# A seven-product output projection in a latent-attention and feed-forward kernel

## The chip, the core and the metric

One core of one Trainium2 chip runs the whole program. The metric is the device time of one execution in microseconds (us). The parts of the core are TensorE (PE, matmuls; PEld is its weight load), VectorE (DVE), ScalarE (ACT), GpSimd (POOL), SyncE (SP, which issues the DMAs here), the on-chip memory SBUF of 128 partitions and the eight accumulator banks of PSUM.

## The reference

For 8 sequences of 512 rows and 512 features (16 heads):

```
h = layernorm(x)
q = rmsnorm(h @ wq_a.T) @ wq_b.T            # latent 384; per head 128 plain + 64 rotary
c, k_pe = split(h @ wkv_a.T); c = rmsnorm(c) # latent 128 + 64 rotary
k, v = split(c @ wkv_b.T)                    # per head 128 + 128
att = softmax((q . [k, rope(k_pe)]) / sqrt(192))
x = x + concat_heads(att @ v) @ wo.T
g = layernorm(x); x = x + (silu(g@gate*s1) * (g@up*s2)) @ down * s3   # weights rounded to fp8, 1536 wide
```

## The kernel before

Each float32 operand of a matmul is split in two f16 halves, high and low, and a product is made of three matmuls (high high, high low, low high: `mul3`, lines 291 to 293). The key and value weights are absorbed once in a setup, so that a head's query (`absorb`, 9 matmuls) meets the latent keys directly, its context is 128 latent values wide (`values`, 12 matmuls, lines 674 to 676) and one matrix per head, `WVO` (128 x 512), takes the context to the output (`project_out`, 4 tiles of 128 rows x 3 matmuls of 512 columns).

The engines run lists written out by hand, held together by semaphores. The batches follow each other: setup, then per batch attention over 16 heads and an FFN of 12 chunks. In `head_step` TensorE does the scores of head i (4 half-height matmuls and 16 full ones, into the four SC banks), the values of head i - 1, the absorption for head i + 2 and the projection of head i - 1. There is one bank, BQ, for absorption. VectorE takes four row maxima (`maxima`), the reciprocals of the sums (`sums_of_head`), splits the context into two halves (`context`), adds the four projected tiles into `XR`, multiplied by the reciprocal of each row's sum (`add_out`, line 1449), and makes the low half of the absorbed query (`qa_lo`). ScalarE makes every exponential twice (`probs`, lines 1077 and 1079): in f32 into `P32`, of which there is one buffer, and in f16 into `PH`; then the high half of the absorbed query (`qa_hi`). GpSimd makes the low halves `PL` = `P32` - `PH` (line 1716), two tiles at a time; the f32 exponentials of the next head wait for it. SP transposes both halves by DMA. The memory of `P32` also holds `YT`, the FFN's output, until GpSimd has added it to the residual (line 1781), at the start of the next batch.

Queries' rotary parts are made in 8 rotations a batch (`rotated_ahead` on TensorE, `rot_products` and `rot_lo` on VectorE, `rotate` on GpSimd, lines 1687 and 1688): 5 beside the FFN before, 3 in the first two heads. At a batch's end (`last_of_attention`) the 8 latents of the next batch (4 of q, 4 of k) fill TensorE's waits: q1, q2, k2 and q3 stand between the last projection and the transposes of the normalised rows (line 557). The last batch has an ending of its own (`end_of_attention`), with 21 filler matmuls (`keep_warm`). The statistics of the next batch's input and its normalised rows (`next_norm`) are made beside heads 3 to 10.

## Time and profile before

| | |
|---|---|
| median of 3 runs | 2231.78 us (2231.71 to 2232.05) |
| the profiled execution | span 2228.8 us; the page gives no other time of it |
| TensorE busy, granted clock | 2205.4 us (99%), 0.999 |
| VectorE, ScalarE, GpSimd busy | 1557.8, 1066.6, 1001.5 us |
| DMA | 219.42 MB, 47.7% of 16 engines in its main queue |

Busy time is a union: overlapping instructions count once. A matmul's own duration (379 ns for 512 columns) is longer than the distance to the next. In timelines and chains the first number is the start from the span's beginning, the second the length.

### The profile page before, as it was taken

What the parts mean: (1) busy time and instruction counts of PE and PEld (TensorE: products, weight loads), DVE (VectorE), ACT (ScalarE), POOL (GpSimd) and SP (SyncE); (2) the same over time, 40 slices, a digit from 0 to 9 for tenths busy, and PEclk for the clock granted to TensorE, in tenths of its full rate; (3) what the DMA queues carried; (4) which work ended last, traced back from release to release, by engine and by line L of the source; (5) the groups of instructions that cost most, each with busy time, mean ns of one, the idle gap of its engine ahead of it and who ended that gap; (6) DMA issues with size and microseconds to landing.
All of it is one profiled execution on the core that took longest, in us unless ns stands there. A gap on an engine that the chain in (4) does not pass through costs nothing.

```text
span 2228.8 us, 34908 instructions
## 1 busy us (share of the span) xinstructions
PE 2205.4 (99%) x10977; PEld 1026.8 (46%) x10977; DVE 1557.8 (70%) x3227; ACT 1066.6 (48%) x2345; POOL 1001.5 (45%) x688
## 2 busy tenths in 40 slices
PE   7999999999999999999999999999999999999999
PEld 5444544445444454444544445444454445444454
DVE  7888887776477764777648775587755877467773
ACT  6667564554255542555325553355443554345532
POOL 4657465453355524454244642536334363343322
PEclk9999999999999999999999999999999999999999
DMA  7868336562175631756216561365614564145530
GB/s 248 188 124 150 88 71 142 106 124 51 23 151 105 122 53 34 145 105 127 44 43 146 106 121 29 73 123 106 118 25 104 106 115 95 24 104 109 106 65 19
DMA packets 703800, 219.42 MB, mean 98 GB/s; under 512 B 685520, under 2 KB 685776, under 8 KB 702672
## 3 DMA queue, kind: packets, MB, share of 16 engines
q1 hardware_dynamic: 703696, 218.09, 47.7%
q8 instruction: 59, 0.97, 0.2%
q14 instruction: 45, 0.37, 0.0%
HBM read 40.78 MB, written 8.39 MB: 22 GB/s over the span
## 4 chain that ended last, share of the span: by engine, by line
PE 93%; DVE 3%; ACT 1%; DMA 1%; POOL 1%; issue 1%; SPq 0%; DVEq 0%; POOLq 0%
PE bank L853 13%; PE bank L291 11%; PE bank L293 11%; PE bank L292 11%; PE scores L863 7%; PE scores L663 5%; PE scores L293 5%; PE scores L291 5%; PE scores L292 5%; PE bank L674 4%; PE bank L675 4%; PE bank L676 4%; PE scores L660 3%; PE bank L840 1%; PE bank L689 1%; PE scores L557 1%
## 5 line engine op out<-in xcount | busy, mean ns | idle before, releaser
L1716 POOL TENSOR_TENSOR arena<-arena 128x1024 f16<-128x1024 f32 x256 | 545.7, 2132 | 620.3 <-ACT arena L1079 620.3
L1077 ACT ACTIVATE arena<-scores,shift 128x512 f32<-128x512 f32 x512 | 357.5, 698 | 535.0 <-DVE shift L1429 494.8
L1449 DVE SCALAR_TENSOR_TENSOR arena<-bank,rden,arena 128x512 f32<-128x512 f32 x508 | 347.9, 743 | 137.0 <-PE bank L293 137.0
L1427 DVE TENSOR_REDUCE mx<-scores 128x1 f32<-128x512 f32 x512 | 352.5, 689 | 20.5 <-PE scores L293 16.7
L1079 ACT ACTIVATE arena<-scores,shift 128x512 f16<-128x512 f32 x512 | 358.6, 700 | 0.0
L853 PE MATMUL bank<-arena,WFF 128*128 128x512 f16 x1392 | 313.5, 379 | 0.8 <-DVE arena L1601 0.6
L1774 POOL TENSOR_TENSOR arena<-arena 128x512 f16<-128x512 f32 x96 | 114.4, 1191 | 255.6 <-ACT arena L1152 255.6
L853 PEld LDWEIGHTS bank<-arena,WFF 128*128 128x128 f16 x1392 | 135.9, 98 | 164.1 <-DVE arena L1601 2.3
L291 PE MATMUL bank<-WVO,arena 128*128 (+1 forms) x512 | 194.2, 379 | 2.4 <-DVE arena L1222 1.2
L1222 DVE SCALAR_TENSOR_TENSOR arena<-bank,arena 128x512 f16<-128x512 f32 (+1 forms) x263 | 176.2, 670 | 29.1 <-ACT arena L1070 24.4
L663 PE MATMUL scores<-arena 128*128 128x512 f16 x512 | 195.4, 382 | 0.0
L292 PE MATMUL bank<-WVO,arena 128*128 (+1 forms) x512 | 194.1, 379 | 0.0
L291 PE MATMUL scores<-arena 128*128 128x512 f16 x512 | 194.0, 379 | 0.0
L292 PE MATMUL scores<-arena 128*128 128x512 f16 x512 | 194.0, 379 | 0.0
L293 PE MATMUL scores<-arena 128*128 128x512 f16 x512 | 194.0, 379 | 0.0
L293 PE MATMUL bank<-WVO,arena 128*128 (+1 forms) x512 | 194.0, 379 | 0.0
L674 PE MATMUL bank<-arena 128*128 128x512 f16 x476 | 180.4, 379 | 1.9 <-DMA arena<-arena 1.7
L676 PE MATMUL bank<-arena 128*128 128x512 f16 x476 | 180.4, 379 | 0.0
L675 PE MATMUL bank<-arena 128*128 128x512 f16 x476 | 180.4, 379 | 0.0
L1441 DVE TENSOR_SCALAR arena<-bank 128x512 f16<-128x512 f32 (+1 forms) x135 | 89.0, 660 | 130.1 <-PE bank L676 125.7
L863 PE MATMUL scores<-WFF,arena 128*128 128x512 f16 x752 | 177.6, 379 | 0.0
L1601 DVE SCALAR_TENSOR_TENSOR arena<-arena,bank 128x512 f32<-128x512 f32 x96 | 65.9, 687 | 158.5 <-ACT arena L1146 158.4
(159 smaller groups left out, 3480.5 us busy)
## 6 DMA issues: line engine op xcount, KB each, us to landing
arena<-arena SPq DMA_TRANSPOSE x712, 3.2
arena<-w_ffn SPq DMA_DIRECT2D x24, 384.0 KB, 3.5
arena<-x SPq DMA_DIRECT2D x8, 1024.0 KB, 5.6
out<-arena SPq DMA_DIRECT2D x32, 256.0 KB, 2.0
arena<-x SPq DMA_DIRECT2D x14, 512.0 KB, 4.4
WVO<-w_o SPq DMA_DIRECT2D x4, 1024.0 KB, 8.2
arena<-w_nope SPq DMA_DIRECT2D x4, 768.0 KB, 9.1
arena<-down_scale SPq DMA_DIRECT2D x8, 256.0 KB, 3.3
```

The lines of the kernel that those rows point to most:

```text
L291: pe.matmul(dst, lhsT=ls(0), rhs=rs(0), start=first, stop=False)
L292: pe.matmul(dst, lhsT=ls(0), rhs=rs(1), start=False, stop=False)
L293: return pe.matmul(dst, lhsT=ls(1), rhs=rs(0), start=False, stop=last)
L663: pe.matmul(dst, lhsT=Q1[:, par, tile(t)], rhs=KA[:, :], start=False, stop=False)
L674: pe.matmul(dst[:, :], lhsT=KV[:, 0, j, :], rhs=PT[:, par, 0, :, j, :], start=(j == 0), stop=False)
L853: m = pe.matmul(dst[:, :], lhsT=w[:, c, k, :], rhs=XT[:, p, k, :], start=(k == 0 and p == 0), stop=(k == NK - 1 and p == 1))
L863: m = pe.matmul(SC[:, t, :], lhsT=FU[:, c % 4, p, tile(t)], rhs=WD[:, c, :], start=(c == 0 and p == 0), stop=(c == NF - 1 and p == 1))
L1077: act.activation(P32[:, t, :], SC[:, t, :], ACT.Exp, scale=EXP_SCALE, bias=shift[:, t:t + 1], accum_out=esum[:, par, t:t + 1]).then_inc(s[ ...
L1079: act.activation(PH[:, par, t, :], SC[:, t, :], ACT.Exp, scale=EXP_SCALE, bias=shift[:, t:t + 1]).then_inc(s["ph"], 1)
L1427: dve.tensor_reduce(mx[:, t:t + 1], SC[:, t, :], AX_X, ALU.max).then_inc(s["mxr"], 1)
L1449: dve.scalar_tensor_tensor(out=XR[:, t, :], in0=banks[t][:, :], scalar=by[:, t:t + 1], in1=XR[:, t, :], op0=ALU.mult, op1=ALU.add).then_in ...
L1716: pool.tensor_tensor(PL[:, par, two, :], P32[:, two, :], PH[:, par, two, :], ALU.subtract).then_inc(s["pl"], 1)
```

## The change

From batch 2 on (`B_PLAIN`), heads 0 to 13 are taken in seven pairs ("duos"). The contexts of a pair (512 rows x 256) times their two matrices (256 x 512) are cut into 2 x 2 blocks and multiplied in seven products of sums of blocks instead of eight (Winograd's form of Strassen's). A product (`duo_product`) is 2 tiles of rows x 3 matmuls of 256 columns. The sums need contexts that are already divided by the row sums, so each head's exponentials are divided: ScalarE makes them once, in f32, then `PH` as a scaled copy and `P32` scaled in place; GpSimd multiplies one tile of four, in heads 0 to 2 two of them (`N_TWO`). GpSimd also sums the blocks of the contexts (`context_sums`, `context_sums_rest`). The sums of the weights' blocks are made in batch 1 by GpSimd and ScalarE (`block_sums`), written to DRAM and loaded for each pair by SP (`early_blocks`, 524 KB, and `late_blocks`, 393 KB); their space on chip is that of `WVO` of heads 0 to 13. The values of head i now come two steps after its scores. Scores wait for `ex`, the f32 exponentials, instead of `ph`. Heads 14 and 15 are projected as before.

Six rotations instead of five are made beside the FFN; of the other two one stays ahead of the scores and one comes after step 1, its halves made by GpSimd (`rotated_halves`). The k latent of tile 2 moves from behind q2 to between the halves of the last values, in all batches but the last. The next input's statistics and rows move, from batch 2's on, to VectorE beside the FFN (`next_norm`, `next_rows`), their halves to ScalarE and GpSimd in heads 4, 6, 8 and 10. The last late weights are issued ahead of one transpose. In the last batch `end_of_attention` interleaves the last two pairs with heads 14 and 15 by halves, and its last down products go tile by tile, tile 3 last; additions of tiles 2 and 3 follow their scaling at once. The FFN's loops, the setup and batches 0 and 1 are otherwise as before.

```diff
+B_PLAIN = 2
...
+EARLY = [(X_E1, W_B11, 0, True), (X_O1, W_B21, 2, True), (X_S1, W_T1, 1, True), (X_S2, W_T2, 0, False)]
+LATE = [(X_S3, W_T3, 0, False), (X_S4, W_B22, 1, False), (X_O2, W_T4, 2, True)]
+ADDS = [(0, 0, 0), (2, 0, 0), (1, 1, 1), (0, 0, 1), (0, 1, 0), (0, 1, 1), (1, 0, 1), (2, 1, 0)]
 CHUNK_ROT = 5
...
-N_ROT_FFN = 5
+N_ROT_FFN = 6
+N_ROT_SETUP = NT + 1
...
+N_TWO = 3
...
-LAST_DOWNS = [(NF - 2, 0), (NF - 2, 1), (NF - 2, 2), (NF - 1, 0), (NF - 1, 1), (NF - 2, 3), (NF - 1, 2), (NF - 1, 3)]
+FIRST_DOWNS = [(NF - 4, 0), (NF - 4, 1)]
+LAST_DOWNS = [(NF - 3, 0), (NF - 3, 1), (NF - 3, 2), (NF - 4, 2), (NF - 2, 0), (NF - 2, 1), (NF - 2, 2),
+              (NF - 1, 0), (NF - 1, 1), (NF - 1, 2), (NF - 4, 3), (NF - 3, 3), (NF - 2, 3), (NF - 1, 3)]
...
+    def duo_head(b, i):
+        if i < NH - 2:
+            sp.wait_ge(s["sp"], NT * (b * NH + i) + NT)
+            rope_rows(i + 2, i % 2)
+        if i == 1:
+            sp.wait_ge(s["rot"], (b + 1) * 2 * N_ROT)
+            sp.sem_inc(s["turn"])
+        if i >= 2:
+            sp.wait_ge(s["ctp"], b * N_CT + i - 1)
+            sp.sem_inc(s["turn"])
+        for half in range(2):
+            prob_rows_hi(b * NH + i, i % 2, half)
+            if half and i == NH - 1:
+                late_blocks(b, N_DUO - 1)
+            prob_rows_lo(b * NH + i, i % 2, half)
...
+    def early_blocks(b, j):
+        if j == 0:
+            sp.wait_ge(s["t_out"], 16 * N_DUO)
+            sp.wait_ge(s["outp"], b * (NH * NT))
+        else:
+            sp.wait_ge(s["outp"], order_of_duo(b, j - 1) + N_EARLY)
+        sp.dma_start(WB[:, :, 0:N_EARLY], w_duo[j, :, :, 0:N_EARLY]).then_inc(s["w_early"], 16)
+    def late_blocks(b, j):
+        if j > 0:
+            sp.wait_ge(s["outp"], order_of_duo(b, j - 1) + 8)
+        sp.dma_start(WB[:, :, N_EARLY:], w_duo[j, :, :, N_EARLY:]).then_inc(s["w_late"], 16)
...
+    def duo_product(j, x, w, bank, start):
+        for t in range(2):
+            dst = bank[:, t * HB:(t + 1) * HB]
+            for m, (p, q) in enumerate(((0, 0), (0, 1), (1, 0))):
+                r = pe.matmul(dst, lhsT=XP[j % 2][:, p, x, tile(t)], rhs=WB[:, q, w, :],
+                              start=(start and t == 0 and m == 0), stop=(m == 2), skip_group_check=True)
+        return r
...
     def end_of_attention(b):
         final = NH // 2 - 1
         scores(b, final, 0)
+        values(b, final - 1, 0)
+        duo_early(b, N_DUO - 2, last=True)
+        scores(b, final, 1)
         values(b, final - 1, 1)
-        scores(b, final, 1)
-        project_out(b, final - 1, 1)
         ph = (b * NH + NH - 1) * NT
-        values_by_halves(b, 0, VBANK_END[0], ((s["qal"], b * NH + NH), (s["outr"], (b * NH + NH - 2) * NT - 1)))
+        values_by_halves(b, 0, (BQ[:, :], BQ[:, :]), ((s["outr"], order_of_duo(b, N_DUO - 2) + 2),))
+        duo_late(b, N_DUO - 2)
         last = ((s["ph"], ph + 1), (s["ph"], ph + 2))
+        values_by_halves(b, 1, VBANK_END[1], last, (0,))
         end_project_out(b, 0, 0)
-        values_by_halves(b, 1, VBANK_END[1], last, (0,))
         end_project_out(b, 0, 1)
+        duo_early(b, N_DUO - 1)
+        pe.wait_ge(s["ph"], ph + NT)
         end_project_out(b, 1, 0)
+        duo_late(b, N_DUO - 1, last=True)
         values_by_halves(b, 1, VBANK_END[1], last, (1,))
         end_project_out(b, 1, 1)
             if t == 2 and final:
...
+    def duo_step(b, i):
+        scores(b, i // 2, i % 2)
+        if i >= 2:
+            values(b, i // 2 - 1, i % 2)
+        if i >= 4 and i % 2 == 0:
+            duo_early(b, (i - 4) // 2, (0,))
+        if i == 5:
+            duo_early(b, 0, (2, 3))
+        absorb(i + 2, b * NH + i + 2)
+        if i >= 4 and i % 2 == 0:
+            duo_early(b, (i - 4) // 2, (1,) if i == 4 else (1, 2, 3))
+        elif i >= 5:
+            duo_late(b, (i - 5) // 2)
...
         absorb(2, base + 2)
-        for n in range(N_ROT_FFN + 1, N_ROT):
+        if b >= B_PLAIN:
+            duo_step(b, 1)
+        for n in range(rot_first(first) + 1, N_ROT):
             rotated_ahead(b, n)
-        head_step(b, 0, 1)
-        if first:
+        if b >= B_PLAIN:
+            for i in range(2, NH - 2):
+                duo_step(b, i)
+        else:
...
+        else:
+            project_out(b, final - 1, 1)
         pe.wait_ge(s["lat"], lat + 1)
         values(b, final, 0, BQ)
+        if b >= B_PLAIN:
+            duo_late(b, N_DUO - 2)
         ph = (base + NH - 1) * NT
         pe.wait_ge(s["ph"], ph + 1)
         latent("k", 0)
         pe.wait_ge(s["ph"], ph + 2)
         latent("k", 1)
         project_out(b, final, 0)
-        last_values(b)
+        if b >= B_PLAIN:
+            duo_early(b, N_DUO - 1)
+        else:
+            last_values(b, 0)
+        pe.wait_ge(s["ph"], ph + 4)
+        latent("k", 2)
+        if b >= B_PLAIN:
+            last_values(b, 0)
+            duo_late(b, N_DUO - 1)
+        last_values(b, 1)
         project_out(b, final, 1)
...
+    def probs_divided(b, i):
+        g, par, n = b * NH + i, i % 2, (b - B_PLAIN) * (2 * N_DUO) + i
+        for t in range(NT):
+            act.wait_ge(s["shift"], NT * g + t + 1)
+            if i > 0 and t % 2 == 0:
+                act.wait_ge(s["pl"], 2 * g - 1 + t // 2)
+            act.activation(P32[:, t, :], SC[:, t, :], ACT.Exp, scale=EXP_SCALE, bias=shift[:, t:t + 1],
+                           accum_out=esum[:, par, t:t + 1]).then_inc(s["ex"], 1)
+        if i == 0:
+            qa_hi(g + 2, 0)
+        for t in range(NT):
+            if t % 2 == 0:
+                act.wait_ge(s["rdn"], 2 * n + 1 + t // 2)
+                if i >= 2:
+                    act.wait_ge(p_t[par][t // 2], halves_landed(b, i))
+            act.wait_ge(s["ex"], NT * g + t + 1)
+            if t == NT - 1 or t == NT - 2 and i < N_TWO:
+                act.wait_ge(s["nm3"], by_pool(b, i, t))
+                act.activation(PH[:, par, t, :], P32[:, t, :], ACT.Copy).then_inc(s["ph"], 1)
+            else:
+                act.activation(PH[:, par, t, :], P32[:, t, :], ACT.Copy,
+                               scale=rden_duo[:, par, t:t + 1]).then_inc(s["ph"], 1)
+                act.activation(P32[:, t, :], P32[:, t, :], ACT.Copy,
+                               scale=rden_duo[:, par, t:t + 1]).then_inc(s["nm"], 1)
...
+    def reciprocals(b, i, halves=range(2)):
+        g, par = b * NH + i, i % 2
+        for half in halves:
+            two = slice(2 * half, 2 * half + 2)
+            dve.wait_ge(s["ex"], NT * g + 2 * half + 2)
+            for t in (2 * half, 2 * half + 1):
+                dve.tensor_scalar(dsum_duo[:, par, t:t + 1], esum[:, par, t:t + 1], 1.0 / NS, None,
+                                  ALU.mult).then_inc(s["dsn"], 1)
+            dve.wait_ge(s["dsn"], ((b - B_PLAIN) * (2 * N_DUO) + i) * 4 + 2 * half + 2)
+            dve.reciprocal(rden_duo[:, par, two], dsum_duo[:, par, two]).then_inc(s["rdn"], 1)
...
+    def context_rows(b, i):
+        n, j, par = b * N_CT + i, i // 2, i % 2
+        dve.wait_ge(s["ctp"], n + 1)
+        k = (b - B_PLAIN) * N_DUO + j
+        if par == 0 and k > 0:
+            dve.wait_ge(s["x_sum"], 5 * k - 1)
+        if par and k > 0:
+            dve.wait_ge(s["x_lo"], k)
+        x = X32[:, X_O1:X_O2 + 1] if par else XE
+        dve.tensor_scalar(x, BC[:, :].rearrange("p (m n) -> p m n", m=2), 1.0 / NS, None,
+                          ALU.mult).then_inc(s["cth"], 1)
...
+    def context_lo(b, i):
+        j, par = i // 2, i % 2
+        dve.wait_ge(s["x_hi"], (b - B_PLAIN) * 2 * N_DUO + i + 1)
+        if par:
+            x = slice(X_O1, X_O2 + 1)
+            split_lo(XP[j % 2][:, 1, x], BC[:, :].rearrange("p (m n) -> p m n", m=2), 1.0 / NS,
+                     XP[j % 2][:, 0, x]).then_inc(s["ctl"], 1)
+        else:
+            split_lo(XP[j % 2][:, 1, X_E1], BC[:, 0:HB], 1.0 / NS, XP[j % 2][:, 0, X_E1]).then_inc(s["ctl"], 1)
...
+    def add_block(b, j, k, bank=None):
+        base = order_of_duo(b, j)
+        if j == 0 and k == 0:
+            dve.wait_ge(s["ld_res"], b * 16 + 16)
+        dve.wait_ge(s["outp"], base + k + 1)
+        if k == 0:
+            dve.wait_ge(s["outr"], base)
+        if k in (1, 7):
+            dve.wait_ge(s["outr"], base + (1 if k == 1 else 5))
+        add_to(k, DBANK[ADDS[k][0]] if bank is None else bank)
...
+    def duo_step(b, i):
+        g = b * NH + i
+        maxima(g)
+        reciprocals(b, i, (0,))
+        if i >= 2:
+            qa_lo(g + 1, 1 - i % 2)
+        reciprocals(b, i, (1,))
+        if i == 2:
+            rot_lo(b, N_ROT_FFN)
+        if i >= 2:
+            context_rows(b, i - 2)
+        if i >= 4 and i % 2 == 0:
+            duo_adds(b, (i - 4) // 2, (0,))
+        if i == 5:
+            duo_adds(b, 0, (2, 3))
+        if i >= 2:
+            context_lo(b, i - 2)
+        if i >= 4 and i % 2 == 0:
+            duo_adds(b, (i - 4) // 2, (1,) if i == 4 else (1, 2, 3))
+        elif i >= 5:
+            duo_adds(b, (i - 5) // 2, (4, 5, 6, 7))
...
-            for t in range(2, NT):
+            if last and t >= 2:
                 dve.wait_ge(s["yt"], b * NT + t + 1)
                 dve.tensor_tensor(XR[:, t, :], XR[:, t, :], YT[:, t], ALU.add).then_inc(s["yv"], 1)
         if not last:
...
+    def head_divided(b, i):
+        g, par, n = b * NH + i, i % 2, (b - B_PLAIN) * (2 * N_DUO) + i
+        pool.wait_ge(s["ex"], NT * g + NT)
+        pool.wait_ge(s["rdn"], 2 * n + 2)
+        for t in (NT - 2, NT - 1) if i < N_TWO else (NT - 1,):
+            pool.tensor_tensor(P32[:, t, :], P32[:, t, :], rden_duo[:, par, t:t + 1].broadcast_to((P, S)),
+                               ALU.mult).then_inc(s["nm3"], 1)
+        if i >= 3 and i % 2:
+            context_sums(b, (i - 3) // 2)
+        if i == 1:
+            rotate(b, N_ROT - 1)
+        for half in range(2):
+            two = slice(2 * half, 2 * half + 2)
+            pool.wait_ge(s["nm"], by_act(b, i, 2 if half and i >= N_TWO else 1))
+            if half:
+                pool.wait_ge(s["nm3"], by_pool(b, i, NT - 1))
+            pool.wait_ge(s["ph"], NT * g + 2 * half + 2)
+            pool.tensor_tensor(PL[:, par, two, :], P32[:, two, :], PH[:, par, two, :],
+                               ALU.subtract).then_inc(s["pl"], 1)
+        if i >= 3 and i % 2:
+            context_sums_rest(b, (i - 3) // 2)
+        if i == 2:
+            rotated_halves(b, N_ROT - 1)
...
+    def rotated_halves(a, n):
+        half, t = n // NT, n % NT
+        heads = slice(half * 8, half * 8 + 8)
+        hi, lo = (slice(DR * o, DR * o + DR) for o in (t % 2, 1 - t % 2))
+        raw = rot_buf(a, n).rearrange("p (h d) -> p h d", h=NH // 2)
+        pool.wait_ge(s["rot"], a * 2 * N_ROT + 2 * n + 2)
+        pool.sem_inc(s["turn"])
+        pool.tensor_copy(QPE[:, heads, t, hi], raw).then_inc(s["qpeh"], 1)
+        pool.wait_ge(s["qpeh"], a * N_ROT + n + 1)
+        pool.tensor_tensor(QPE[:, heads, t, lo], raw, QPE[:, heads, t, hi], ALU.subtract).then_inc(s["qpel"], 1)
...
+    def context_sums(b, j):
+        k, n = (b - B_PLAIN) * (5 * N_DUO) + 5 * j, b * N_CT + 2 * j
+        def step(to, x, y, op, after):
+            if after:
+                pool.wait_ge(s["x_sum"], k + after)
+            pool.tensor_tensor(to, x, y, op).then_inc(s["x_sum"], 1)
+        pool.wait_ge(s["cth"], n + 2)
+        x = [X32[:, m] for m in range(N_BLK)]
+        step(x[X_S1], XE[:, 1], x[X_O2], ALU.add, 0)
+        step(x[X_S3], XE[:, 0], XE[:, 1], ALU.subtract, 0)
+        step(x[X_S2], x[X_S1], XE[:, 0], ALU.subtract, 1)
+        step(x[X_S4], x[X_O1], x[X_S2], ALU.subtract, 3)
+    def context_sums_rest(b, j):
+        k = (b - B_PLAIN) * (5 * N_DUO) + 5 * j
+        pool.wait_ge(s["outp"], b * (NH * NT) + max(0, 8 * j - 8))
+        pool.wait_ge(s["x_sum"], k + 4)
+        pool.sem_inc(s["turn"])
+        pool.tensor_copy(XP[j % 2][:, 0, X_S3:], X32[:, X_S3:]).then_inc(s["x_sum"], 1)
+        pool.wait_ge(s["x_sum"], k + 5)
+        pool.tensor_tensor(XP[j % 2][:, 1, X_S3:], X32[:, X_S3:], XP[j % 2][:, 0, X_S3:],
+                           ALU.subtract).then_inc(s["x_lo"], 1)
+    def attention(b, last, first, plain):
```

## Rows read from the trace of the kernel before

**Rows 1.** The page, part 1: busy us (share of the span) xinstructions.

```profile
PE 2205.4 (99%) x10977; PEld 1026.8 (46%) x10977; DVE 1557.8 (70%) x3227; ACT 1066.6 (48%) x2345; POOL 1001.5 (45%) x688
```

**Rows 2.** Who TensorE waited for: us in total, times, longest.

```profile
PE scores L557 <- DVE arena L1301: 10.5, 1, 10.5
PE bank L674 <- DMA arena<-arena: 1.7, 2, 1.2
```

**Rows 3.** The chain of waits, batch 2: start us, us, what.

```profile
808.95 3.49 PE bank L840 x32
812.45 6.91 PE bank L853 x32
```

**Rows 4.** Timeline of PE: setup, a head, a batch's end, the next one's start.

```profile
10.52 3.65 PE L557 MATMUL scores<-ident,arena 128*128 128x128 f32 x16 [10.52 <-DVE arena L1301]
...
704.13 0.61 PE L660 MATMUL scores<-arena 64*128 64x512 f16 x4
...
715.35 0.61 PE L660 MATMUL scores<-arena 64*128 64x512 f16 x4
...
806.00 1.08 PE L557 MATMUL scores<-ident,arena 128*128 128x128 f32 x8
...
886.62 0.60 PE L660 MATMUL scores<-arena 64*128 64x512 f16 x4
```

**Rows 5.** Timeline of DVE in that head.

```profile
705.75 0.69 DVE L1427 TENSOR_REDUCE mx<-scores 128x1 f32<-128x512 f32 x1
706.47 0.15 DVE L1429 TENSOR_SCALAR shift<-mx 128x1 f32<-128x1 f32 x1
706.61 0.69 DVE L1427 TENSOR_REDUCE mx<-scores 128x1 f32<-128x512 f32 x1
...
711.65 0.69 DVE L1222 SCALAR_TENSOR_TENSOR arena<-bank,arena 128x512 f16<-128x512 f32 x1
713.60 2.73 DVE L1449 SCALAR_TENSOR_TENSOR arena<-bank,rden,arena 128x512 f32<-128x512 f32 x4 [1.25 <-PE bank L293]
```

**Rows 6.** Groups of POOL by line and form: busy us, mean ns | idle before.

```profile
L1716 POOL TENSOR_TENSOR arena<-arena 128x1024 f16<-128x1024 f32 x256 | 545.7, 2132 | 620.3 <-ACT arena L1079 620.3
...
L1737 POOL TENSOR_SCALAR arena<-arena,mv,rs_x 128x512 f32<-128x512 f32 x28 | 58.0, 2073 | 0.0
...
L1687 POOL TENSOR_TENSOR arena<-arena 128x256 f32<-128x256 f32 x64 | 54.7, 854 | 84.0 <-DVE arena L1370 79.1 <-DVE arena L1380 4.8
...
L1781 POOL TENSOR_TENSOR arena<-arena 128x512 f32<-128x512 f32 x30 | 37.1, 1268 | 42.6 <-DVE arena L1641 42.6
...
L1741 POOL CAST arena<-arena 128x512 f16<-128x512 f32 x24 | 14.6, 609 | 4.1 <-POOL arena L1737 4.1
...
L1708 POOL TENSOR_TENSOR arena<-arena 128x512 f16<-128x512 f32 x8 | 9.3, 1158 | 1.2 <-ACT arena L1032 1.2
```

**Rows 7.** Timeline of POOL at the start of batch 3.

```profile
884.34 4.94 POOL L1781 TENSOR_TENSOR arena<-arena 128x512 f32<-128x512 f32 x4 [5.84 <-DVE arena L1641]
```

**Rows 8.** Timeline of ACT there.

```profile
889.41 0.69 ACT L1077 ACTIVATE arena<-scores,shift 128x512 f32<-128x512 f32 x1 [5.76 <-POOL arena L1781]
...
894.83 0.68 ACT L1037 ACTIVATE arena<-arena 128x512 f16<-128x512 f32 x1
```

**Rows 9.** Timeline of DVE at the end of batch 2.

```profile
797.46 0.74 DVE L1449 SCALAR_TENSOR_TENSOR arena<-bank,rden,arena 128x512 f32<-128x512 f32 x1
...
798.85 0.73 DVE L1449 SCALAR_TENSOR_TENSOR arena<-bank,rden,arena 128x512 f32<-128x512 f32 x1
...
805.31 1.92 DVE L1301 TENSOR_SCALAR arena<-arena,mv,rs_y 128x512 f32<-128x512 f32 x4
```

**Rows 10.** Timeline of DVE: batch 3's start and the program's end.

```profile
897.86 1.06 DVE L1380 TENSOR_TENSOR arena<-arena 128x512 f16<-128x512 f32 x1
...
2224.16 1.98 DVE L1646 TENSOR_TENSOR arena<-arena 128x512 f32<-128x512 f32 x2
```

**Rows 11.** Busy us by engine in a stretch, then PEclk, DMA share, GB/s: the end.

```profile
2226.00:2229.00 3.00, 0.00 (x0) 0.00 (x0) 0.14 (x1) 0.00 (x0) 0.00 (x0) 0.56 0.65 247
```

553 lines of the change are left out of this document (438 added, 115 removed).

## The prediction

> **What bounds the kernel now.** I read the busy shares first: TensorE 99%, VectorE 70%, ScalarE 48%, GpSimd 45% [rows 1]. Then who TensorE waited for: 10.5 us once, in the setup, and under 2 us for anything else [rows 2]. So TensorE's columns set the time, and everything else is hidden behind them. The chain of waits gives their price: 32 matmuls of 512 columns in 6.91 us, 0.2159 each; 32 of 256 columns in 3.49 us, 0.1091 each [rows 3]. Half-width matmuls cost half. Last I read one head, engine by engine [rows 4 to 6], to see how long each would need if it had to follow another, and the end and start of a batch [rows 4, 7 to 9].
>
> **What the change saves.** Two heads' projection is now 2 x 4 x 3 = 24 matmuls of 512 columns: 24 x 0.2159 = 5.18 us. In seven products it is 7 x 2 x 3 = 42 of 256 columns: 42 x 0.1091 = 4.58. That is 0.60 us a pair, 4.2 us in a batch of seven pairs, and 25.2 us in the six batches 2 to 7. One rotation of each batch moves into the FFN before it: TensorE does it at either place, so it costs nothing by itself. All other TensorE work stays.
>
> **What it adds off TensorE, for a pair of heads** (new time 2 x 11.22 - 0.60 = 21.8 us; 11.22 = 715.35 - 704.13, of which 33 matmuls of values, absorption and projection are 7.12 and the scores with the pause ahead of them 4.1 [rows 3, 4]).
> - GpSimd: four differences of 1024 elements, 4 x 2.13; two multiplications of 512 by the reciprocal; four sums of 256 elements; one copy and one difference of 1024 [rows 6]. No row has such a multiplication: the nearest is the f32 addition of 512, 1.27; bounds 0.61 (a copy) and 2.07 (the two-scalar operation). I take 1.27. The sums of 256: 0.85 with stride two in the rows, 0.6 half of 1.27; I take 0.65. Total 8.5 + 2.5 + 2.6 + 3.3 = 17.0 of 21.8 us (was 8.5 of 22.4).
> - ScalarE: eight exponentials instead of sixteen, but then eight copies and six scalings from SBUF at about 0.57 apart (the copy in the rows is 0.68 long, and instructions overlap by some 0.1 [rows 8]), and two halves of the contexts: 8 x 0.68 + 14 x 0.57 + 1 + 1.2 = 15.6 us.
> - VectorE: reductions and shifts as before (0.86 a tile), eight additions, four small steps more per head: about 18 us [rows 5].
> - DMA: 0.9 MB of weights a pair, about 42 GB/s more. They are issued a pair ahead of their use; I cost them at nothing. If the cover went, each late load would show as a wait of TensorE before the first or fifth product. In batch 1 GpSimd makes the block sums, some 9 us a pair of the 13.9 it is idle: nothing too.
>
> In the middle of a batch this fits. The closest wait is for the low half of the next head's absorbed queries: VectorE has four maxima by 1.5 + 4 x 0.86 = 5.0 us after the scores begin, the first reciprocals at 5.4, the half at 6.1; TensorE has done scores (4.1) and values (2.6) at 6.7. Half a microsecond of slack.
>
> **Where it doesn't fit: the start of each batch.** P32, the f32 exponentials, is one buffer, and its use is now longer. Head g + 1 may not write tiles 0 and 1 before GpSimd's first difference of head g, nor 2 and 3 before the second; the difference comes after the divisions, these after all four exponentials. From the second difference to the next head's second: 1.5 (two exponentials, 0.68 apart and then read out) + 0.5 (reciprocals: three dependent steps of 0.15 [rows 5]) + 2.5 (two multiplications, heads 0 to 2) + 4.3 = 8.9 us, and 10.2 at an odd head with the sums. TensorE's work per head there is less: no projection, so scores, values and absorption are 8.6 us, and heads 0 and 1 are only 6.0 and 8.0 us long. Followed from the first scores (0): exponentials can't begin before GpSimd's residual additions end, at 2.8 [rows 4, 7, 8]; head 0's are done at 6.0, reciprocals 6.6, two multiplications 9.1, differences 11.3 and 13.4. Head 1: exponentials 15.0, reciprocals 15.5, multiplications 18.0, the last rotation (0.85 + 0.8, put between) 19.7, first difference 21.8. Head 2: two exponentials 23.4, reciprocals 23.9, and only then, in VectorE's order, the low half for head 3: 24.6. TensorE: 6.0; 14.0; it waits 0.5 for head 1's last exponentials; scores to 18.6, values to 21.2, and then it needs that low half, because the absorption of head 4 takes the same bank: it waits until 24.6, **3.4 us**. By the same steps the next absorptions wait 0.7 and 1.1, and the second product of the first pair 1.2 (context low half behind head 4's reciprocals). Sum 0.5 + 3.4 + 0.7 + 1.1 + 1.2 = **6.9 us** a batch. After head 5 the projection's products lengthen TensorE's steps to 21.8 a pair against 19 to 20 for the chain, and the waits end. Bounds: with the multiplication at 0.61 the sum is 5.0, at 2.07 it is 12.8; with the multiplication at 1.16 and every other step at the lower of its rows, 5.7.
>
> One thing may stretch this. VectorE's rotation difference took 1.06 us beside a GpSimd operation where its usual is 0.68 [rows 10], and one stands in this chain at head 2. The Trainium skill ("SBUF — State Buffer", section "Who interferes with whom") has a VectorE instruction with two SBUF inputs and a GpSimd one exclude each other for the whole instruction. By that rule the chain would be up to 0.4 us longer a batch; the row agrees in size. I leave it out of the sum.
>
> **The batch's end.** The k latent of tile 2 (12 matmuls of 192 columns, by the rate of rows 3 about 12 x 0.082 = 0.99 us) is moved ahead of the last values. It filled the wait for the layer norm: the first normalised tile was ready at 805.31 + 0.54 and the transposes began at 806.00 [rows 4, 9], so there is 0.1 us to spare. VectorE's chain gets shorter by overlap of its additions and statistics, 3 x (1.39 - 1.27) = 0.35 [rows 9]. So 0.99 - 0.10 - 0.35 = 0.55 us of new waiting in each of batches 0 to 6; with the pair's products there, 0.8 in batches 2 to 6.
>
> **The last batch.** Start as above, +6.9 - 4.2. Its attention's end is bound by the same steps as before (half contexts, then the norm): 0 +- 1.5, taken as 0.3 for the first matmuls of head 15. At the very end the additions of tiles 2 and 3 no longer wait for all four scalings and tile 3's eight matmuls come last: one addition of 1.0 leaves the tail [rows 10]. Sum +2.0.
>
> **Sum.** Batches 2 to 6: 6.9 + 0.8 - 4.2 = +3.5 each, 17.5. Last +2.0. Batches 0 and 1 +1.1. Total **+20.6 us**: span 2228.8 to 2249.4. The page's execution has only its span; the median of the runs is 3.0 above it, so 2231.8 becomes 2252.
>
> **Rivals.**
> - *The columns win*: the waits at the start stay under the 4.2 us saved. For it: the middle of the batch fits, and TensorE waited for nothing before. It decides where the multiplication and the chain around it are some 3 us shorter than my rows. If they vanish: 2231.8 - 25.2 + 1.1 - 1.0 = 2206.7. Against: the differences alone (4 x 2.13 in heads 0 and 1) are half of the chain and are measured.
> - *The multiplication by a broadcast column costs what the two-scalar operation costs*, 2.07: +5.9 a batch, 2287. Against: the other two-input operations are all at 1.2 to 1.3.
> - *The clock falls in the wait.* After the last matmul the granted clock is at 0.56 of 2.4 GHz over the last 3 us, so it went to 1.2 GHz within them [rows 11], and the first 16 transposes took 3.65 us where 8 take 1.08 later [rows 4], 1.5 too much. A wait of 3.4 us could bring that in six batches: +9, 2261. Against: the wait is a single one, with dense work on both sides. The Trainium skill ("TensorE: Matmul & The Clock Gate", Part 1) says that an idle stretch brings the array to 1.2 GHz; by that rule a price like this is due in some of the batches, and the trace's first matmuls agree.
> - *A slack of 0.5 us too few in the middle*: every head pays. A tenth each over 72 heads is +7.
>
> **Chances.** Forecast, waits at the start outweigh the columns: 0.67, its own range 2240 to 2265. Clock or thin slack on top: 0.07. Costly multiplication: 0.03. The columns win: 0.18. The two cancel: 0.05. About 0.2% (4.5 us) is what a measurement can tell. Faster 0.18, same 0.05, slower 0.77. Range 2222 to 2272, which leaves most of the faster case out.
>
> **What would show it.** TensorE waiting for VectorE before the first matmul of head 4's absorption, 3 us in each of six batches, and GpSimd's differences back to back there; seven products at 0.109 a matmul; no waits in heads 6 to 13; a wait of half a microsecond at the transposes of each batch. Wrong if TensorE's idle time is under 4 us a batch.

## The result, and the profile after

The changed kernel takes 2249.66 us (2249.30 to 2251.35, 4 runs), the kernel before 2231.74 (4 runs): ratio 1.0082, 95% interval 1.0067 to 1.0096. It is slower, by more than a measurement of this kernel leaves open. The profiled execution has a span of 2247.5 (before 2228.8), so 18.7 us are to be found.

Part 1 of its page (busy us, share of the span, instructions), to be held against [rows 1]:

```profile
PE 2189.5 (97%) x11732; PEld 1100.3 (49%) x11732; DVE 1589.8 (71%) x3581; ACT 1283.4 (57%) x2688; POOL 1361.8 (61%) x1083
```

TensorE has less work (15.9 us less busy) and more idle time: 58.0 us where it had 23.4. Who it waited for (us in total, times, longest; before: [rows 2]):

```profile
PE bank L347 <- DVE arena L1551: 20.8, 20, 2.4
PE scores L695 <- DVE arena L1630: 13.4, 9, 10.1
PE bank L911 <- issue: 5.9, 6, 1.0
PE bank L822 <- DMA arena<-arena: 4.5, 5, 1.5
PE bank L347 <- DVE arena L1781: 2.3, 1, 2.3
PE scores L800 <- ACT arena L1339: 1.7, 6, 0.3
```

L347 behind L1551 is the absorption behind the low half of an absorbed query, L911 the pair products, L822 the values. L695 are the transposes of normalised rows: 10.1 us of theirs is the setup's wait, which was there before. The timeline of PE in batch 3 shows where they lie (start, length, what; the idle time before an instruction in brackets):

```profile
895.44 0.61 PE L800 MATMUL scores<-arena 64*128 64x512 f16 x4
901.48 0.61 PE L800 MATMUL scores<-arena 64*128 64x512 f16 x4
909.46 0.85 PE L800 MATMUL scores<-arena 64*128 64x512 f16 x3
910.59 0.39 PE L800 MATMUL scores<-arena 64*128 64x512 f16 x1 [0.28 <-ACT arena L1339]
...
919.37 0.39 PE L347 MATMUL bank<-arena,WAB 128*128 128x512 f16 x1 [2.24 <-DVE arena L1551]
...
928.63 0.39 PE L347 MATMUL bank<-arena,WAB 128*128 128x512 f16 x1 [0.46 <-DVE arena L1551]
...
938.77 0.39 PE L347 MATMUL bank<-arena,WAB 128*128 128x512 f16 x1 [0.67 <-DVE arena L1551]
941.91 0.81 PE L911 MATMUL bank<-WVO 128*128 128x256 f16 x6 [1.02 <-issue]
...
976.40 0.61 PE L800 MATMUL scores<-arena 64*128 64x512 f16 x4
...
998.25 0.60 PE L800 MATMUL scores<-arena 64*128 64x512 f16 x4
...
1086.22 1.08 PE L695 MATMUL scores<-ident,arena 128*128 128x128 f32 x8 [0.43 <-DVE arena L1630]
```

Five waits at the start of the batch, none in the middle, one at the end. The pair in the middle (scores 976.40 to scores 998.25) takes 21.85, where two heads took 2 x 11.22 [rows 4]: the 0.6 us a pair are there. A wait costs more than its idle time, because a matmul's own 0.38 is longer than the 0.216 to the next one; counted as the distance beyond the usual, the five are 0.69 (the 0.28 and a gap hidden in the merged line above it), 2.41, 0.62, 0.84 and 1.19, together 5.75 a batch.

Where the 18.7 us are, from the first transposes of each batch's end (L557 before, L695 after) to the next:

| stretch | before | after | difference | predicted |
|---|---|---|---|---|
| setup and batch 0 | 262.98 | 262.37 | -0.6 | +0.55 |
| batch 1 | 271.80 | 276.82 | +5.0 | +0.55 |
| batches 2 to 6 | 1355.84 | 1367.04 | +11.2 | +17.5 |
| batch 7 and the end | 338.18 | 341.27 | +3.1 | +2.0 |

The first line says nothing by itself: in the runs below, which leave the setup as it is, it lies anywhere from 262.2 to 265.0.

GpSimd's timeline at the start of batch 3 is the chain that the prediction followed:

```profile
901.86 2.04 POOL L2283 TENSOR_TENSOR arena<-arena,rden_duo 128x512 f32<-128x512 f32 x2 [2.18 <-DVE rden_duo L1805]
904.78 4.21 POOL L2295 TENSOR_TENSOR arena<-arena 128x1024 f16<-128x1024 f32 x2 [0.89 <-ACT arena L1355]
911.07 2.04 POOL L2283 TENSOR_TENSOR arena<-arena,rden_duo 128x512 f32<-128x512 f32 x2 [2.07 <-DVE rden_duo L1805]
913.06 0.85 POOL L2181 TENSOR_TENSOR arena<-arena 128x256 f32<-128x256 f32 x1
913.86 0.85 POOL L2182 TENSOR_TENSOR arena<-arena 128x256 f32<-128x256 f32 x1
914.66 4.22 POOL L2295 TENSOR_TENSOR arena<-arena 128x1024 f16<-128x1024 f32 x2
920.95 2.40 POOL L2283 TENSOR_TENSOR arena<-arena,rden_duo 128x512 f32<-128x512 f32 x2 [2.07 <-DVE rden_duo L1805]
923.93 4.21 POOL L2295 TENSOR_TENSOR arena<-arena 128x1024 f16<-128x1024 f32 x2 [0.58 <-ACT arena L1355]
```

Multiplications, differences, and between them 2 us in which GpSimd itself waits: for reciprocals, these for exponentials, these for GpSimd's own last difference. The same circle on ScalarE (head 2's exponentials) and VectorE (its reciprocals, then the low half that TensorE waits for):

```profile
916.83 0.69 ACT L1339 ACTIVATE arena<-scores,shift 128x512 f32<-128x512 f32 x1 [1.81 <-POOL arena L2295]
...
918.31 0.21 DVE L1802 TENSOR_SCALAR dsum_duo<-esum 128x1 f32<-128x1 f32 x2 [2.86 <-ACT arena L1339]
...
918.64 0.67 DVE L1551 SCALAR_TENSOR_TENSOR arena<-bank,arena 128x512 f16<-128x512 f32 x1
```

It is a circle through one buffer, not an engine at its limit.

### The profile page after: what moved, and what is told of

Same layout as the page of the kernel before. It is cut to its first block, busy times and chain, and to the rows that moved or that the text cites. A ratio compares the mean times of both kernels' runs of the same rounds, so it can differ in the third digit from the quotient of the medians.

```text
span 2247.5 us, 37427 instructions
## 1 busy us (share of the span) xinstructions
PE 2189.5 (97%) x11732; PEld 1100.3 (49%) x11732; DVE 1589.8 (71%) x3581; ACT 1283.4 (57%) x2688; POOL 1361.8 (61%) x1083
## 3 DMA queue, kind: packets, MB, share of 16 engines
q8 instruction: 90, 1.47, 0.3%
## 4 chain that ended last, share of the span: by engine, by line
PE 77%; DVE 7%; POOL 5%; ACT 4%; issue 4%; DMA 1%; SPq 1%; ACTq 0%; POOLq 0%; DVEq 0%
PE bank L1098 13%; PE bank L911 8%; PE scores L1108 7%; PE bank L347 6%; PE bank L349 6%; PE bank L348 6%; PE scores L803 4%; PE scores L349 4%; PE scores L348 4%; PE scores L347 4%; PE bank L822 4%; PE bank L823 4%; PE bank L824 4%; POOL arena L2295 3%; PE scores L800 2%
## 5 line engine op out<-in xcount | busy, mean ns | idle before, releaser
L1339 ACT ACTIVATE arena<-scores,shift 128x512 f32<-128x512 f32 x336 | 230.0, 686 | 191.5 <-DVE shift L1765 98.7
L1847 DVE SCALAR_TENSOR_TENSOR arena<-bank,arena 128x512 f32<-128x512 f32 x336 | 216.9, 687 | 74.0 <-PE bank L911 73.2
L911 PE MATMUL bank<-WVO 128*128 128x256 f16 x1764 | 213.5, 273 | 6.1 <-issue 5.9
L911 PEld LDWEIGHTS bank<-WVO 128*128 128x128 f16 x1764 | 171.7, 98 | 53.4 <-DVE arena L1817 8.7
L347 PE MATMUL scores<-arena 128*128 128x512 f16 x512 | 194.0, 379 | 0.0
L2283 POOL TENSOR_TENSOR arena<-arena,rden_duo 128x512 f32<-128x512 f32 x102 | 107.4, 1060 | 132.8 <-DVE rden_duo L1805 132.8
L1327 ACT ACTIVATE arena<-scores,shift 128x512 f32<-128x512 f32 x176 | 122.5, 696 | 110.4 <-DVE shift L1765 104.7
L822 PE MATMUL bank<-arena 128*128 128x512 f16 x476 | 180.4, 379 | 4.7 <-DMA arena<-arena 4.5
L1474 ACT ACTIVATE arena<-bank,gsc 128x512 f32<-128x512 f32 x96 | 65.7, 684 | 190.2 <-PE bank L1098 174.2
L1353 ACT ACTIVATE arena<-arena,rden_duo 128x512 f16<-128x512 f32 x234 | 166.5, 712 | 0.0
```

What stands on the lines that cost most here:

```text
L347: pe.matmul(dst, lhsT=ls(0), rhs=rs(0), start=first, stop=False)
L822: pe.matmul(dst[:, :], lhsT=KV[:, 0, j, :], rhs=PT[:, par, 0, :, j, :], start=(j == 0), stop=False)
L911: r = pe.matmul(dst, lhsT=XP[j % 2][:, p, x, tile(t)], rhs=WB[:, q, w, :], start=(start and t == 0 and m == 0), stop=(m == 2), skip_group_ ...
```

## The experiments

Each is timed against the kernel before (2230.9 to 2231.7 in these sets). All but one change the changed kernel.

**The order of VectorE.**

```diff
 maxima(g)
-reciprocals(b, i, (0,))
 if i >= 2:
     qa_lo(g + 1, 1 - i % 2)
+reciprocals(b, i, (0,))
 reciprocals(b, i, (1,))
```

> In the changed kernel, VectorE makes the low half of the next absorbed query ahead of the head's first reciprocals, in every step of the paired batches. Theory (the single buffer of f32 exponentials sets the start of a batch, VectorE's order only names the place of the wait): the low half for head 3 is then made right behind the four maxima of head 2 (915.45 in batch 3), so the wait of 2.23 us before head 4's absorption goes, but the scores of head 3 need head 2's last exponentials (920.34) and the second product needs the context of head 2, both at the same time as now. The waits of 0.46 and 0.68 move there too. Idle time of TensorE per batch as now, about 4.7 us; time 2249.7, within 1.5. Rival (VectorE's order is the cause): the waits of 2.23, 0.46 and 0.68 go and nothing takes their place: 3.4 us in six batches, 20 us, 2229.

Measured: 2257.91, ratio 1.0121 (1.0104 to 1.0137). The rival is out: the three waits before the absorptions went, and others took their place: 0.3 to 0.5 at the scores, behind exponentials, and above all 3.04 at the second product of the first pair. PE's timeline there:

```profile
942.93 0.82 PE L911 MATMUL bank<-WVO 128*128 128x256 f16 x6 [3.04 <-issue]
```

The theory had the places and the sum right: in batch 3 the second product starts 46.45 us after the batch's first scores, 46.47 in the changed kernel. It missed 8 us, which come behind that product. The stretch there says why (busy us by engine; then PEclk, DMA share, GB/s):

```profile
944.00:947.50 3.50, 3.50 (x12) 1.20 (x9) 1.32 (x3) 2.55 (x6) 3.50 (x2) 0.51 0.85 101
```

The granted clock is 0.51, 1.2 GHz, for 3.4 us (6.8 in one batch), in each of the six batches. A batch takes 274.65 to 275.15, and 276.2 with the long one, where it took 273.35: 1.3 to 1.8 us for a fall of 3.4. So the prediction's rival "the clock falls in the wait" is a real mechanism, at a wait of 3.04 (2.93 in the last batch). At the 2.24 us of the changed kernel it fell in one of six batches.

**A second buffer for head 1.**

```diff
+def f32_of(i):
+    return XR if i == 1 else P32
 ...
+P32 = f32_of(i)
 ...
-    if i > 0 and t % 2 == 0:
-        act.wait_ge(s["pl"], 2 * g - 1 + t // 2)
+    if i == 1 and t == 0:
+        act.wait_ge(s["stored"], b * (16 * NT))
+    elif i > 1 and t % 2 == 0:
+        act.wait_ge(s["pl"], 2 * g - 1 - (2 if i == 2 else 0) + t // 2)
```

> In the changed kernel, head 1's f32 exponentials of the paired batches go to a memory of their own: XR, which holds the residual rows only from the load behind head 1's last difference. Head 1's exponentials wait for the last output rows to be stored instead of head 0's differences, head 2's for head 0's differences instead of head 1's. Theory (single buffer): head 1's exponentials start behind head 0's copies, 10.2 us after the first scores, and are done at 13.1 instead of 15.0; its multiplications end at 15.7, the last rotation at 17.4, the differences at 21.6; head 2's exponentials have been made meanwhile, so its multiplications end at 23.6 and its second difference at 27.8, where it was 32.7. 4.9 us less in the chain, of which up to 5.7 of waiting is there to be taken back: minus 27 to 29 us over six batches, time 2221 to 2223. The waits before the absorptions of heads 4 and 5 go, those before head 6's (0.7) and before the second product (1.0) stay. Rival (GpSimd's amount of work, not its waiting for the exponentials, sets the start): only the 1.9 us by which head 1's exponentials come sooner, minus 11 us, 2238. Rival (the buffer is not what matters, VectorE's order is): 2249.

Measured: 2225.56, 0.9974 (0.9964 to 0.9984): 24.1 us less than the changed kernel, and faster than the kernel before. The waits left in batch 3:

```profile
930.17 0.39 PE L350 MATMUL bank<-arena,WAB 128*128 128x512 f16 x1 [0.29 <-DVE arena L1557]
933.31 0.81 PE L914 MATMUL bank<-WVO 128*128 128x256 f16 x6 [1.02 <-issue]
```

The single buffer was the cause of the long wait and of most of the start's loss. A batch takes 269.19: 4.16 less, not 4.9. Head 2's second difference ends 28.5 us after the first scores (27.8 expected, 32.7 in the changed kernel). The wait of 1.02 at the second product is not the buffer's length: it is the same here and in the next run. There the low half of the absorbed query releases TensorE's absorption, and the context's low half, which the product needs, ends 3.09 us later in VectorE's order, with head 4's second reciprocals between them (938.71 to 941.80 in the changed kernel, 930.11 to 933.20 here).

**No division.** ScalarE's scalings in place and GpSimd's multiplications are left out, and the waits for them; ScalarE makes a plain copy `PH` per tile.

> In the changed kernel, the exponentials of the paired heads are not divided by the sums: ScalarE makes four exponentials and four copies per head, no scaling in place, GpSimd makes no multiplication, the differences wait for the copies alone. The output is that of undivided contexts. All of TensorE's work, the sums of blocks, the weight loads and the adds stay. Theory (the division lengthens the chain through the one buffer beyond TensorE's step): from one head's second difference to the next's there are then 1.5 + 0.6 + 4.3 = 6.4 us, less than TensorE's 8.6 at the start; nearly all of the 5.75 us of waiting a batch goes, 34 us in six batches: 2215 to 2218. The seven products then show their 25 us. Rival (something else in the changed TensorE order, as late weights or the bank order, makes the waits): 2240 or more.

Measured: 2231.03, 0.9999 (0.9990 to 1.0008), 13 us above the range and 9 below the rival. The waits shrink to 1.09 and 0.21, and the 1.02 at the second product stays. What holds the first of them is in GpSimd's timeline:

```profile
899.90 4.21 POOL L2286 TENSOR_TENSOR arena<-arena 128x1024 f16<-128x1024 f32 x2 [3.67 <-ACT arena L1349]
907.55 0.84 POOL L2179 TENSOR_TENSOR arena<-arena 128x256 f32<-128x256 f32 x1 [3.44 <-DVE arena L1704]
908.35 0.84 POOL L2180 TENSOR_TENSOR arena<-arena 128x256 f32<-128x256 f32 x1
909.14 4.21 POOL L2286 TENSOR_TENSOR arena<-arena 128x1024 f16<-128x1024 f32 x2
```

Head 1's differences (909.14) stand behind the last rotation (907.55), whose products VectorE makes only behind head 1's reciprocals. With the division that wait is hidden under the multiplications. Neither theory had it: the moved rotation is a link of the chain with a time of its own. This is read from the trace; no run without the division moved the rotation.

**The k latent back behind q2.**

```diff
-LATENTS = [("q", 0), ("k", 0), ("k", 1), ("k", 2), ("q", 1), ("q", 2), ("q", 3), ("k", 3)]
+LATENTS = [("q", 0), ("k", 0), ("k", 1), ("q", 1), ("q", 2), ("k", 2), ("q", 3), ("k", 3)]
...
-pe.wait_ge(s["ph"], ph + 4)
-latent("k", 2)
...
 latent("q", 2)
+pe.wait_ge(s["ph"], ph + 4)
+latent("k", 2)
...
```

> In the changed kernel, the k latent of tile 2 is put back behind the q latent of tile 2, where it was in the kernel before. Theory (it was the filler of TensorE's wait for the layer norm): the wait of 0.43 us ahead of the transposes, 0.48 longer than the 0.11 of before in pace, goes in each of the seven batches that have it: minus 3.4 us, 2246.3. Rival (the norm's chain alone sets the transposes and the place of the latent is free): 2249.7, within 1.

Measured: 2247.13, 1.0071 (1.0057 to 1.0084): 2.5 us less. The wait at the transposes is gone. Four of the batches 2 to 6 take 0.55 less (272.8 for 273.35; batch 2 273.13 for 273.68), and batch 4 0.2, with a new wait of 0.30 before one of its products. The theory holds, with a part of it given back elsewhere.

**Heads 1 and 3 in XR.** As for head 1 alone, with the load of the residual rows behind head 3.

> In the changed kernel, the f32 exponentials of heads 1 and 3 of the paired batches go to XR (in the run before only head 1's), and the residual rows are loaded behind head 3's last difference. Theory (single buffer): with head 1 alone in XR, 0.2 + 0.46 + 1.18 us of waiting a batch were left, all behind the exponentials of heads 3 and 4; these now wait for head 1's and head 2's differences and come in time. About 1.5 us less in each of six batches than 2225.6: 2216, within 2.5. Rival (a transfer takes the wait's place): head 3's last difference ends about 37 us after the first scores, the load of 1 MB takes 5.9 us, and the first addition into XR is due at about 43; it comes later, the product banks stay full and TensorE waits for them: 2224 or more.

Measured: 2268.26, 1.0168 (1.0154 to 1.0182). The rival, and worse than it: SP comes to the load behind head 3's transposes, and the second product waits for the first addition. SP's line for the load in batch 3, VectorE's for the first addition, PE's for the product, and the window around it:

```profile
939.01 0.41 SPq L590 DMA_DIRECT2D arena<-x  x1
```

```profile
944.71 0.69 DVE L1855 SCALAR_TENSOR_TENSOR arena<-bank,arena 128x512 f32<-128x512 f32 x1 [7.37 <-DMA arena<-x]
```

```profile
945.83 1.44 PE L916 MATMUL bank<-WVO 128*128 128x256 f16 x6 [6.63 <-issue]
```

```profile
942.60:949.40 6.80, 3.57 (x13) 1.30 (x14) 1.71 (x3) 0.00 (x0) 3.58 (x3) 0.50 1.21 258
```

All other waits of this batch's start are gone, and one of 6.63 us has come (6.18 to 7.28 in the six batches), with the clock at 1.2 GHz for 6.8 us in each, from inside the wait on.

**The rotation behind the differences.**

```diff
-if i == 1:
-    rotate(b, N_ROT - 1)
 for half in range(2):
     ... differences ...
+if i == 1:
+    rotate(b, N_ROT - 1)
```

> In the changed kernel, GpSimd makes the last rotation behind head 1's differences instead of between its multiplications and its differences. Theory (everything in that chain counts): the first difference of head 1 (914.66 in batch 3) then waits only for ScalarE's scaling, which ends at 912.98, so it comes 1.5 us sooner; the wait before head 4's absorption falls from 2.23 to 0.8, the others stay: minus 8 to 9 us in six batches, and the one fall of the clock goes too (1.7): 2239 to 2242. Rival (the rotation is later and SP holds head 1's transposes for it, 3 us later, so the values of head 1 wait): no gain, 2250.

Measured: 2250.81, 1.0088 (1.0074 to 1.0102). Both came true at once:

```profile
919.16 0.39 PE L347 MATMUL bank<-arena,WAB 128*128 128x512 f16 x1 [0.72 <-DVE arena L1551]
928.00 0.38 PE L822 MATMUL bank<-arena 128*128 128x512 f16 x1 [2.62 <-DMA arena<-arena]
```

The wait for the low half fell to 0.72, and the values of head 1 wait 2.62 for transposes that SP holds back until the rotation is read: its products lie in `TRG`, whose memory is the second half of `PT`, where these transposes go. The rotation can't be moved there alone. The six waits for these values are 2.38 to 2.69; the clock fell for 3.4 us behind two of them (2.68 and 2.46) and not behind 2.69, 2.63, 2.62 and 2.38. The two batches with a fall take 274.35 and 273.90, the other three of batches 2 to 6 272.5 to 272.8.

**A longer wait.**

```diff
 if i == 1:
+    pool.tensor_tensor(extra[:], WVO[:, NH - 1, 0, 0:272], WVO[:, NH - 1, 1, 0:272], ALU.add)
     rotate(b, N_ROT - 1)
```

> In the changed kernel, GpSimd makes one more addition of 272 elements, into memory that nobody reads, ahead of the last rotation in head 1 of each paired batch, about 0.7 us. Theory A (the wait before head 4's absorption grows one for one, and a single wait of about 3 us brings the clock down to 1.2 GHz for 3.4 us, as it did in each batch where VectorE's order had gathered the waits into one of 3.04 us, and as it did in one batch of six at 2.23 us): 6 x 0.7 = 4.2, and 1.7 us in each of five more batches, 8.5: 2262. Theory B (the clock fell there for another reason than the wait's length, as the place or the narrow products behind it): 4.2 us alone, 2254.

Measured: 2254.48, 1.0104 (1.0088 to 1.0119). The number is B's, the mechanism is A's: the clock did fall, in four of the six batches (behind 2.88 three times and 3.01, not behind 2.81 and 2.89). PE's wait in one of them, and the stretch behind it:

```profile
920.78 0.39 PE L348 MATMUL bank<-arena,WAB 128*128 128x512 f16 x1 [2.88 <-DVE arena L1552]
```

```profile
921.90:925.30 3.40, 3.40 (x11) 0.78 (x10) 1.96 (x6) 2.87 (x6) 2.40 (x2) 0.50 0.85 149
```

That batch takes 273.99, and batch 6, which has no fall, 273.98. The fall costs nothing here: TensorE would have waited for the chain before the next absorptions anyway (0.46 and 0.67 in the changed kernel, 0.45 and 0.69 here in a batch without a fall, none with one), and the slow matmuls fill these waits. Where the wait is the last of the start, as in the first experiment, nothing takes it up.

**All together, first try.** Heads 1 and 3 in XR, the k latent back, and batch 1's block sums on GpSimd five and five, in two steps.

> The changed kernel with heads 1 and 3 in XR, with the k latent of tile 2 back behind q2, and in batch 1 with GpSimd's block sums split over two steps (five operations in each, their low half in the step after), where ten of them and the next rows' half (7.5 + 1.2 us) stood beside 4.25 us of differences in a step of 11.2. Theory: 2216 as with the two heads alone, 2.5 less by the latent as measured, and of the waits for transposed exponentials in batch 1 those at heads 9 and 11 go (0.70 + 0.87): 2212, within 2.5. Rival (the parts stand in each other's way, or ScalarE's half of the block sums now comes between head 14's exponentials and its latents): above 2216.

Measured: 2266.30, 1.0156 (1.0142 to 1.0170), for the residual load of the run with two heads. Of use is batch 1 alone: 274.29 us instead of 276.26 in that run, 0.3 to 0.55 by the latent (276.50 in the run with it alone, 276.82 in the changed kernel), the rest, some 1.5, by the split sums.

**One rotation, in the kernel before.** `N_ROT_FFN = 6` from batch 1 on, two rotations in the first heads.

> In the kernel before, only the rotation moves: six of the eight of each batch are made beside the FFN before it, from batch 1 on, and two in the first two heads. Theory (the third rotation was TensorE's cover for the way from head 0's exponentials over GpSimd's low halves and SP's transposes to its values, as batch 1 of the changed kernel shows with 1.63 us of waiting before those values instead of 0.23, and 0.55 before the first projection): about 1.9 us in each of seven batches, plus 13 us, 2245. If only the first of the two waits comes, 1.4 each: 2241. Rival (what the prediction said: a rotation costs the same at either place): 2231.7.

Measured: 2243.60, 1.0055 (1.0042 to 1.0069): 12.7 us for moving TensorE work of unchanged amount. A batch from 2 to 6 takes 272.9 to 273.4 instead of 271.0 to 271.5. Who TensorE waited for:

```profile
PE bank L678 <- DMA arena<-arena: 12.9, 10, 1.9
```

These are the values behind transposed exponentials; their line in [rows 2] (L674) has 1.7 us. The rival, which is the prediction's own sentence, is out.

**The parts that held.** Head 1 in XR, the latent, the split sums.

> The changed kernel with head 1 alone in XR (2225.6 when done by itself), the k latent of tile 2 back behind q2 (minus 2.5 by itself), and batch 1's block sums split over two steps (batch 1 took 1.5 us less with it, beside 0.5 by the latent). Theory (three places that have nothing to do with each other): 2225.6 - 2.5 - 1.5 = 2221.6, within 1.5. Rival (some of it overlaps): 2224 or more.

Measured: 2218.24, 0.9943 (0.9929 to 0.9957). By the medians 3.4 us better than the sum of the parts, but the kernel before was 0.8 faster in this set, and the two profiled executions differ by 5.0 (2222.7 and 2217.7), 1.0 more than the parts' 4.0. A batch takes 268.5 to 268.9. So about 1 us is left, and its cause is open.

**With batch 1's rotations back.** `rot_first(b)` is 5 for batches 0 and 1, 6 from batch 2 on, in each engine's list.

> The kernel of the run before (head 1 in XR, k latent back, block sums split; 2218.2) with batch 1 given its old rotations back: five beside the FFN of batch 0 and three in the first heads, six and two from batch 2 on. Theory (batch 1 has plain heads, whose first values need the third rotation as cover, as the kernel before showed with plus 12.7 us over seven batches; the paired batches take head 0's values two steps later and need none): 1.8 us less, 2216.5, within 1.2. Rival (batch 1's first waits have another cause, as the stores of weight blocks that SP issues there): 2218.

Measured: 2217.45, 0.9938 (0.9924 to 0.9951). Batch 1 takes 271.58 instead of 273.88: its first waits, before head 0's values (1.47) and before head 2's (0.46), were the rotation's, and both are gone. The time shows 0.8 of it, within what two such sets can tell; in the profiled execution the clock falls once at the end of the last batch, which takes 1.2 longer. This is the fastest version, 13.5 us under the kernel before. It still waits at the start of paired batches, up to 1.27 before values and 0.5 to 1.0 at the second product.

**One multiplication instead of two.** `N_TWO = 0`.

> In the changed kernel, GpSimd multiplies one tile instead of two in heads 0 to 2 too; ScalarE makes the other one's two scalings. Theory (the differences of heads 0 and 2 wait for ScalarE's scaling of the first two tiles anyway, 904.62 and 923.78 in batch 3; only head 1's stand behind GpSimd's own work): head 1's first difference comes 0.8 us sooner, the wait of 2.23 becomes 1.4, the rest stays: minus 5 us, 2244.7, within 1.5. Rival (each of the three multiplications of 1.04 counts): minus 3.1 a batch, 2231.

Measured: 2245.22, 1.0062 (1.0049 to 1.0076). As the theory has it, 4.4 us less: the wait of 2.24 becomes 1.52, the others stay. Two of the three extra multiplications were hidden by ScalarE.

## Why the prediction was right, and where it was not

The forecast was 2252, with the waits at the start of each batch outweighing the columns; the time is 2249.66. The mechanism is shown, by the trace and by the run with a second buffer. That the number came within 2.3 us is partly luck, because errors of both signs cancel: batches 2 to 6 were put 6.3 too high, batch 1 was 4.5 and the last batch 1.1 too low.

- *The columns*: 0.60 a pair, 25.2 us. Right; 21.85 for the pair in the middle against 22.44.
- *The waits at the start*: 0.5, 3.4, 0.7, 1.1, 1.2 predicted, in this order and behind these steps; 0.69, 2.41, 0.62, 0.84, 1.19 measured. The sum of 6.9 a batch was 1.15 too much, which is 6.9 us over six batches. The large one is off by 1.0. Its terms: exponentials of head 0 at 5.8 (6.0), multiplications 8.5 (9.1), differences 13.5 (13.4), head 1's exponentials 15.0 (15.0), multiplications 17.7 (18.0), rotation 19.3 (19.7), the low half 23.9 (24.6). The multiplication takes 1.02 to 1.06, not 1.27. At head 0 that gave nothing: the differences wait there for ScalarE's scaling (0.89 in the rows above), which the prediction's chain left out. The other 0.3 is TensorE, which would have come to the absorption at 21.5, not 21.2. A slip beside it: 1.5 + 0.5 + 2.5 + 4.3 is 8.8, not 8.9; the times followed step by step don't use it.
- *The batch's end*: 0.48 a batch, as the distance beyond the usual. It stands in front of the transposes of batches 0 and 1 too (0.42 and 0.43 of idle time), so 0.55 was near there, though batch 0's own time can't show it; 0.8 in the paired batches was too much, since the pair's products add no wait there.
- *The moved rotation "costs nothing by itself"*: wrong. TensorE's own time is the same at either place, but in batch 1, with plain heads, it was the cover between head 0's exponentials and its values, and SP's transposes come too late without it. PE in batch 1:

```profile
359.15 0.38 PE L822 MATMUL bank<-arena 128*128 128x512 f16 x1 [1.47 <-DMA arena<-arena]
```

  2.3 us by the run that gave it back, which is this wait and the one before head 2's values (0.45 at 382.75). The paired batches take head 0's values two steps later and have no such wait.
- *Block sums "nothing" in batch 1*: wrong by some 1.5. The sum over a pair of heads was right (9.3 us of work), but ten operations stood in one step: 7.2 for them, 1.1 for the next rows' half, 4.2 of differences, 12.5 in a step of 11.2. GpSimd, and PE's waits that follow:

```profile
452.73 1.16 POOL L2243 TENSOR_TENSOR arena<-arena 128x512 f16<-128x512 f32 x1
453.84 4.22 POOL L2210 TENSOR_TENSOR arena<-arena 128x1024 f16<-128x1024 f32 x2
```

```profile
462.01 0.38 PE L822 MATMUL bank<-arena 128*128 128x512 f16 x1 [0.54 <-DMA arena<-arena]
...
485.32 0.38 PE L822 MATMUL bank<-arena 128*128 128x512 f16 x1 [0.71 <-DMA arena<-arena]
```

  With the latent's place, these two are all of batch 1's 5.0 us: with the three put back it takes 271.58, and 271.80 in the kernel before.
- *The last batch*: +3.1, not +2.0. Its start is as in the others. At the attention's end the contexts are 1.1 later than before (2.26 of waiting at 2170.26 where 1.14 stood), and the last stretch gave 0.5 more instead of 1.0 less, by waits before the first gates. This is read from the trace only; no run tried it.
- *DMA* at nothing: no wait for weights in any batch. Right.
- *The shared port*, up to 0.4 left out: in the rows above GpSimd's two multiplications took 2.04 twice and 2.40 at head 2, where VectorE's rotation difference (920.78, 0.67 long, two inputs in SBUF) had begun just before them. The Trainium skill ("SBUF — State Buffer", section "Who interferes with whom") has the two exclude each other; the trace agrees in size, with the delay on GpSimd's side.
- *Rivals*. The columns did not win, as the chain was not 3 us shorter. The multiplication is at 1.06, so 2.07 is out. The clock's fall came once in six batches, in batch 2, and cost nothing that can be seen: batch 2 takes 0.33 more than the others, but 0.35 and 0.37 more in the runs with the k latent back and with one multiplication, where its clock does not fall. The runs show that the rival was near: with 0.7 us more of waiting the fall came in four of six, at 3.04 in all.

## What to carry to other kernels

When work moves off the bottleneck engine, add up the circle through each buffer that has only one copy, at the place where the bottleneck's steps are shortest: here seven products save 25 us in the steady part and lose 34 in the first five heads of each batch, and a buffer that lies idle there for other reasons turns most of the loss back and, with three small repairs, the result into a gain of 13.5. Count a helper's load by step, not by pair, and treat work of the bottleneck engine as cover for what runs beside it before calling its move free. Gathering several small waits into one is no gain, even at the same sum: it can bring the clock down.

## What the runs showed of the hardware that was not expected

- A single wait of TensorE of 2.24 us, in dense work, was followed by 3.4 us at 1.2 GHz in one batch of six; 2.4 to 2.7 in two of six; 2.8 to 3.0 in four of six; 3.04 in all; 6.63 came with 6.8 us, in all. The length alone doesn't decide it: 2.46 had a fall and 2.69 none, and the wait of 2.25 at the end of the last batch's attention, the same in all twelve versions of the changed kernel, was followed by a fall in five of their profiled executions. Such a fall cost 1.3 to 1.8 us where nothing waited behind it and nothing where TensorE was ahead of a chain anyway, so the mean clock of a run (0.996 in one of the changed kernel's runs, 0.999 in another of the same time) says little about its time.
- GpSimd's f32 multiplication of 512 elements by a broadcast column takes 1.04, less than its f32 addition of 512 in place [rows 6], 1.27; its operations of 256 in the sums of blocks take 0.67 to 0.73. By group:

```profile
L2283 POOL TENSOR_TENSOR arena<-arena,rden_duo 128x512 f32<-128x512 f32 x102 | 107.4, 1060 | 132.8 <-DVE rden_duo L1805 132.8
...
L2330 POOL TENSOR_TENSOR WVO<-arena 128x256 f32<-128x256 f32 x42 | 30.6, 729 | 0.0
```
